# Four transfers issued ahead of seven small ones at the start of a one-core kernel

## The reference

```
def _qlora_linear(x, q, scale, bias, la, lb):
    w = _dequant(q, scale)                      # q / 7.5 - 1, times the group's scale
    base = jnp.einsum('btd,od->bto', x, w) + bias
    lora = jnp.einsum('btr,or->bto', jnp.einsum('btd,rd->btr', x, la), lb)
    return base + lora
```

## Time and profile before

| | us |
|---|---|
| median of 3 runs | 616.52 (616.03 to 617.02) |
| the profiled execution's own time | 616.88 |
| its span | 615.2 |
| PE busy in the span | 590.7 (96%) |
| DVE busy | 526.9 (86%) |
| ACT busy | 402.8 (65%) |
| POOL busy | 373.9 (61%) |

### The profile page before, as it was taken

One profiled execution on the slowest core, in us unless ns is written; L12 is line 12 of the kernel. 1 busy time (PEld: TensorE's weight loads), 2 busy tenths in 40 slices (PEclk: granted clock), 3 DMA queues, 4 the chain that ended last, 5 costly groups with the idle time before them and its releaser, 6 DMA issues.

```text
span 615.2 us, 10218 instructions
## 1 busy us (share of the span) xinstructions
PE 590.7 (96%) x3285; PEld 498.3 (81%) x3285; DVE 526.9 (86%) x1164; ACT 402.8 (65%) x619; POOL 373.9 (61%) x361
## 2 busy tenths in 40 slices
PE   6999999999999999999999999999999999999986
PEld 5778879778897889868797788978889688987865
DVE  3679899798888989889897988979898898989797
ACT  2776656848667577766768576684876667775552
POOL 5745766557644766457665575556754576746574
PEclk9999999999999999999999999999999999999999
DMA  9103000500032000500004000230004000030001
GB/s 241 62 2 136 1 2 35 170 2 0 1 125 80 0 0 18 180 6 0 0 35 170 0 0 0 87 118 0 0 0 173 32 0 0 34 102 1 0 2 69
DMA packets 11461, 29.00 MB, mean 47 GB/s; under 512 B 2593, under 2 KB 4273, under 8 KB 11441
## 3 DMA queue, kind: packets, MB, share of 16 engines
q1 hardware_dynamic: 10960, 28.35, 13.7%
q10 hardware_dynamic: 480, 0.41, 0.3%
HBM read 20.37 MB, written 8.39 MB: 47 GB/s over the span
## 4 chain that ended last, share of the span: by engine, by line
PE 70%; ACT 9%; POOL 7%; DVE 6%; issue 6%; DMA 1%; ACTq 1%; DVEq 0%; POOLq 0%
PE bank L1478 19%; PE bank L1484 9%; PE bank L1594 7%; PE bank L1605 7%; PE bank L1649 6%; PE bank L1551 4%; PE bank L1616 4%; PE bank L1570 3%; ACT fw L630 3%; POOL gl L262 2%; ACT L630 2%; PE bank L1578 2%; PE bank L1561 2%; PE bank L1538 2%; PE bank L1471 2%
## 5 line engine op out<-in xcount | busy, mean ns | idle before, releaser
L262 POOL TENSOR_TENSOR gl<-fw,gh 128x512 fp32r<-128x512 f32 x80 | 104.2, 1319 | 49.4 <-DVE gh L937 37.5
L417 POOL TENSOR_TENSOR sqs<-fw 128x512 f32<-128x512 f32 x48 | 62.8, 1309 | 73.8 <-ACT fw L620 73.7
L620 ACT ACTIVATE fw<-bank,b1c 128x512 f32<-128x512 f32 x96 | 62.3, 686 | 57.8 <-PE bank L1484 57.8
L630 ACT ACTIVATE fw<-fw,vec 128x512 f32<-128x512 f32 x96 | 74.6, 808 | 14.2 <-DVE fw L923 13.9
L923 DVE SCALAR_TENSOR_TENSOR fw<-bank,b1c,rb 128x512 f32<-128x512 f32 x96 | 67.7, 745 | 16.1 <-ACT rb L626 15.8
L267 POOL TENSOR_TENSOR hTl<-hT,hTh 128x512 fp32r<-128x512 f32 x40 | 54.1, 1368 | 39.8 <-ACT hTh L639 33.0
L392 POOL TENSOR_TENSOR rsf<-vef,neghalf 128x4 f32<-128x4 f32 x48 | 50.6, 1055 | 43.7 <-DVE vef L914 43.0
L1605 PE MATMUL bank<-K,XN 128*128 128x256 f32 x256 | 61.7, 382 | 0.0
L1649 PE MATMUL bank<-M,qT 128*128 128x256 f32 x256 | 59.4, 379 | 0.0
L392 POOL TENSOR_TENSOR rs<-ve,neghalf 128x2 f32<-128x2 f32 (+1 forms) x48 | 41.9, 874 | 22.8 <-DVE ve L1020 17.1
L1605 PEld LDWEIGHTS bank<-K,XN 128*128 128x128 f32 x256 | 46.5, 190 | 7.6 <-DVE K L982 2.0
(11 more groups left out here) (157 smaller groups left out, 1593.0 us busy)
## 6 DMA issues: line engine op xcount, KB each, us to landing
X<-in_L_attn_x_dram SPq DMA_DIRECT2D x16, 512.0 KB, 6.7
RES<-in_L_attn_x_dram SPq DMA_DIRECT2D x16, 512.0 KB, 4.3
out_dram<-RES SPq DMA_DIRECT2D x14, 512.0 KB, 2.7
XNB<-in_L_ffn_qweights_dram SPq DMA_DIRECT2D x2, 512.0 KB, 6.6
out_dram<-RES SPq DMA_DIRECT2D x4, 256.0 KB, 2.1
RES<-in_L_ffn_qweights_dram SPq DMA_DIRECT2D x1, 512.0 KB, 8.8
Y<-in_L_ffn_lora_a_dram ACTq DMA_DIRECT2D x4, 96.0 KB, 6.6
Wp<-in_L_attn_Wq_dram SPq DMA_DIRECT2D x1, 256.0 KB, 7.6
```

Of the source, the lines that this page charges most:

```text
L262: engine.tensor_tensor(gl[:, h, m, :], fw[:, h, m, :], gh[:, h, m, :].bitcast(F32), ALU.subtract).then_inc(g_low[h][m], 1)
L417: pool.tensor_tensor(sqs[:, h, :], fw[:, h, 0, :], fw[:, h, 1, :], ALU.add).then_inc(sqs_ready[h], 1)
L620: act.activation(fw[:, h, m, :], FB[h][m][:], ACT.Square, bias=b1c[:, m, j:j + 1]).then_inc(sq_ready[h], 1)
L630: act.activation(fw[:, h, m, :], fw[:, h, m, :], ACT.Gelu, bias=lnb[:, m, j:j + 1], scale=lng[:, m, j:j + 1]).then_inc(g_ready[h], 1)
```

## The change

`head` of ACT calls the two loaders in the other order. The loaders themselves are as before, so the wait for `consts`, which stands at the start of `load_vectors`, now comes behind the four transfers of A.

```
             def head():
+                load_lora()
                 load_vectors()
-                load_lora()
                 ln1_normalise(0, 0, None)
```

## The result

| | before | after |
|---|---|---|
| median, us | 616.68 (8 runs, 616.03 to 617.45) | 618.29 (8 runs, 616.91 to 619.13) |
| ratio after / before | | 1.0022 (95%: 1.0013 to 1.0031) |
| profiled execution, us | 616.88 | 618.86 |
| its span, us | 615.2 | 617.1 |

The kernel became slower by 0.22%, 1.4 us (0.8 to 1.9 by the interval); the two medians lie 1.6 us apart. The forecast was a gain of 1.1 us.

A forecast was written before the change was run, and what follows sets the result against it. PE's wait for A in the first 13 us was taken as the bound. Losing its 1.62 us, with vectors landing at 11.1, starts the low-rank part at 12.05, not 13.11: 616.52 - 1.1 = 615.4 us, range 614.5 to 617.1.

The forecast's parts named there:

- What bounds the kernel: First 13 us: A's last transfer holds PE's first low-rank matmul at 13.11; PE idles 1.62 us, all behind moves equally.
- B's delay: DMA ahead of B: one or two early transfers of A, 0.40 us each, make B 0.4 to 0.8 later than 5.84.
- The 24 constants taken as a fixed 3.62 us: PE behind B: B's landing sets when the constants end, so `vec_transpose` moves from 10.21 to 10.6 to 11.0.
- the forecast gain: Low-rank part on PE starts at 12.05 against 13.11: 1.06 us gained, taken as 1.1 for the whole kernel.
- Check 1: DVE reaches `weight_mean` at 13.6; the mean is ready at 14.5, ACT wants it at 14.63, so it just fits.
- v: Start of `vec_transpose` on PE, forecast 11.1 us when the vectors land; low-rank part at v + 0.95, `weight_mean` at v + 2.50.
- The order in which transfers are served: DMA queues: transfers served about in order of issue across both queues, since A had not moved by 7.5 us.
- `x` late: Rival, chance 0.13: A delays `x` by 1.6 us, gain 0 (616.5); half that delay gives 0.8; time 615.7 to 616.5.
- the 11.8 that the prediction had named as a sign of being wrong: XNB's L435 ending after 11.8 us would show `x` or the codes arriving late.
- The vectors: ACT's seven vectors, issued behind A, last at 4.5, land at 11.1; PE's new wait ahead of `vec_transpose` up to 0.9 us.
- the first rival: Chance 0.12: vectors bound PE ahead of `vec_transpose` from v = 12.16, each microsecond beyond costs one; 616.9 to 617.4.
- The slower side: Whole kernel slower by over 0.2%, 617.75 or more: chance 0.06, only from late vectors with scatter.

The follow-up runs named there:

- The run with the bridge: Changed kernel with 8 more constant matmuls ahead of the transposes of B, the 24 behind kept; 616.86 us, ratio 1.0004.
- the kernel with the filled waits: Changed kernel with 32 constant matmuls ahead of B's transposes, 8 before and 8 behind the vectors' transposes; 616.70 us, ratio 0.9997.
- the first experiment: Changed kernel with all 32 constant matmuls ahead of the transposes of B instead of 8 ahead and 24 behind; 616.59 us, ratio 1.0013.

## Why the prediction was wrong

- **What bounds the kernel, and that the rest moves as a block: right.** The head is on the path, A's wait went, and 590.2 us follow as before.
- **B's delay: the step that failed.** The prediction priced each early transfer by its bytes, 0.40 us, and took B's landing from 5.84 to at most 6.64. In the trace B starts PE at 7.73 instead of 5.99, 1.74 us later. Bytes alone don't give it: one early transfer costs `x` 0.98 us and B 0.65, two cost B 1.67. What makes up the rest stays open. The landing itself scatters: with at least one transfer of A issued at 0.79 us beside `x`, `x` landed at 5.97 to 6.39 in six traces.
- **The 24 constants taken as a fixed 3.62 us: the larger miss.** They took 5.13, behind an idle of 2.20 us. The run with the bridge shows it: nearly the same B, an idle of 0.42, 2.84 us, and most of the loss is gone. With it the late B costs nothing that the runs can tell (ratio 1.0004, 0.9995 to 1.0014), but the forecast gain is not there either. What sets the speed of the constants is shown in part only, as the kernel with the filled waits says.
- **Check 1 looked at the wrong reader, and that alone would have cut the gain.** DVE's six copies end at v + 2.50, which the trace confirms (13.46 + 2.50 = 15.96). I tested that against `weight_mean` only. L1471 waits for them too, and starts at 16.01 behind an idle of 0.46. With the forecast's own v = 11.1 it would have started at about 13.65 against 14.08 before: a gain of 0.4 us and not of 1.1. Of the rest of the way, to a loss of 1.4, B and the constants are the reason: they put v at 13.46.
- **The order in which transfers are served: wrong.** From A not moving until 7.5 us I had concluded that all goes about in the order of issue. With A's first issue beside that of `x`, ACT's queue had moved 0.22 MB by 6 us, when `x` had just landed, though only the first 0.1 MB was issued ahead of `x`; by 7.5 us it was 0.35 beside SP's 1.04. The Trainium skill's rule in DMA: Bandwidth & Descriptors (Queues, rings and completion order), that a DMA engine takes turns between queues that have work, is what this trace agrees with. It was given 0.13, as a delay of `x`; the same turns may well have acted on B. They don't settle the price: with two transfers early less of A went by, and B was as late. Why A did not get its turn before the change, with SP's backlog ahead of it, was not settled either.
- **`x` late: that rival came true in part.** `x` was 0.92 us late, and L435 ended at 11.98, behind the 11.8 that the prediction had named as a sign of being wrong. In the changed kernel this was hidden behind B and the constants. In the first experiment it is what PE waits for (until 11.98), and L1719 is 0.77 us earlier than before, about the 0.8 that this rival gave for half of the delay.
- **The vectors: undecided, and not clear of the rival.** The last one was issued at 5.08, the forecast said 4.5: A's issues took 2.07 us and not 1.83, and 4.5 was below the 4.7 that the old pace gave. In the changed kernel nothing waited for them, as L1676 started at 13.46. In four kernels with A issued as in the changed one and `vec_transpose` free earlier, PE waited for them until 10.24, 10.93, 11.60 and 12.50 (forecast 11.1). The last is beyond the 12.16 from which they bound the kernel by the prediction's sum, so the first rival was not far off.
- **The slower side.** The forecast had "slower" at 0.06 and put it all on the vectors. The right place was one row up: in the earlier trace rows the wait of 0.46 us for B stands directly ahead of 24 matmuls, so B had no slack at all. The loss comes from this chain of two errors, a later B and slower constants.

## What to carry to other kernels

A transfer that is moved to the front is paid for by the first transfers of the other queue, and here by more than its bytes. Look which of those has no slack, and put the moved one behind it. Here A behind the codes on SP's own queue came in time and left B and the constants as they were; with 16 constants the kernel was then faster by 0.16%. Matmuls that only keep TensorE busy had no fixed duration here, so a wait ahead of them can be paid twice, and shortening one wait can open another behind which the clock falls. When a piece of work starts later, ask of every reader of its result, and not only of the nearest one, whether it can still be on time.

## What the runs showed of the hardware

- The constant matmul (128x128, f32) ran at two speeds: 24 took 5.13 us (214 ns each) behind a wait of 2.20 us and 2.84 us (118 ns each) behind one of 0.42, a factor of 1.8. The granted clock reads 1.00 in both, so the profile's column did not show this one. In the kernel before, PE changed speed in the middle of the 24: 4 or 5 ran in each half microsecond from 7 to 8.5 us, and 6 or 7 from 8.5 to 10. After waits of 0.87, 1.11, 1.49, 2.12 and 4.89 us ahead of them the 24 took 5.19, 4.58, 4.87, 4.47 and 4.76 us, after 0.46 and 0.51 us 3.62 and 3.71: not in proportion to the wait. Without a wait, 24 took 3.1 us in one kernel and 3.5 in two, but in one execution 4.4 (32 in 6.43, less 2.07 for the first 8), close to the 4.47 behind a wait of 2.12. So a wait of 0.87 us or more ahead went with a long stretch at the slow speed each time, and was not needed for one. The Trainium skill (TensorE: Matmul & The Clock Gate, Part 1) has TensorE start at 1.2 GHz and rise to 2.4 GHz once it has been busy; the two speeds agree with that, the column doesn't.
- Where a trace shows the granted clock fall, at 13 to 14 us in two kernels, two waits stood ahead (1.88 and 1.44 us, 1.91 and 1.09 us) with only the 0.26 us of L1676 between them. The clock was 0.82 and 0.84 from 12 to 14 us and 0.50 from 14 to 16, and eight transposes took 1.91 us instead of 1.04. In one kernel with waits of 0.91 and 1.48 us the mean clock was below 0.998 in five of 12 executions. The kernel before is not free of it: in later series it was 0.996 or less in two of 27 and three of 23 runs, which took 619.2 to 619.8 us.
